# Projection stage cut on two engines, values 17 wide, and the first two attention units scored inside it

## The reference

```python
qkv = einsum('bysd,ed->byse', x, w_qkv) + b_qkv      # 8 batches, 512 tokens, 16 heads of 16
q, k, v = split(qkv.reshape(B, S, 16, 48).transpose(0, 2, 1, 3), 3, axis=-1)
attn = softmax(einsum('bhqd,bhkd->bhqk', q, k) / sqrt(16), axis=-1)
vals = einsum('bhqk,bhkd->bhqd', attn, v)
out  = vals.transpose(0, 2, 1, 3).reshape(B, S, 256) @ w_out.T + b_out
```

## Time and profile before

| what | value |
|---|---|
| runs | 1296.78 us median of 3 (1296.37 to 1297.04) |
| profiled execution | 1293.25 us, its span 1291.2 us |
| mean granted TensorE clock | 0.962 |
| projection: first matmul, last matmul on qk or values | 12.27 us, 98.5 us |
| attention: first score by query, first score by key | 109.60 us, 130.78 us |
| end of attention's last TensorE work | 520.9 us |
| the rest (recurrence, routing, experts) | to 1291.2 us |

### The profile page before, as it was taken

How to read it: one execution, slowest core, us unless ns; L and a number is a source line. 1 busy time by engine, 2 the same in 40 slices (tenths; PEclk the granted TensorE clock), 3 DMA queues, 4 the chain that set the end, 5 groups by cost and what they waited for, 6 DMA issues and landing times. The chain is left out here.

```text
span 1291.2 us, 21179 instructions
## 1 busy us (share of the span) xinstructions
PE 1179.1 (91%) x5606; PEld 704.0 (55%) x5607; DVE 832.4 (64%) x1458; ACT 496.1 (38%) x867; POOL 404.7 (31%) x520
## 2 busy tenths in 40 slices
PE   6996999999999999767999999982999999999996
PEld 3652233333333332454566665551888888888885
DVE  4998788888888883367777788856333433333332
ACT  2430777777777778211212121242122222222221
POOL 1021431101101110211444333446344554455443
PEclk9996999999999999878999999996999999999999
DMA  9885233333333321022334323311133333333332
GB/s 287 309 275 184 71 99 93 103 96 96 100 92 97 103 85 34 33 55 77 98 98 97 70 51 75 82 34 33 30 53 49 49 51 55 49 49 49 53 53 33
DMA packets 108674, 113.04 MB, mean 88 GB/s; under 512 B 26080, under 2 KB 97904, under 8 KB 107600
## 3 DMA queue, kind: packets, MB, share of 16 engines
q1 hardware_dynamic: 90528, 89.05, 24.0%
q0 software_dynamic: 18112, 23.57, 10.6%
HBM read 68.81 MB, written 43.62 MB: 87 GB/s over the span
## 5 line engine op out<-in xcount | busy, mean ns | idle before, releaser
L637 DVE TENSOR_REDUCE neg_max<-by_query 128x2 f32<-128x1024 f32 x256 | 301.3, 1219 | 62.5 <-PE by_query L538 61.7
L696 ACT ACTIVATE k_wu_e<-by_key 128x512 f32<-128x512 f32 x512 | 277.2, 600 | 83.5 <-PE by_key L546 80.0
L546 PE MATMUL by_key<-k_wg_e 99*128 99x512 bf16 x512 | 179.2, 384 | 3.8 <-ACT k_wu_e L696 2.1
L538 PE MATMUL by_query<-k_wg_e 96*128 96x512 bf16 x512 | 160.4, 396 | 11.3 <-PEq L106 7.5
L1407 POOL DMA_INDIRECT out_rows<-y,slot x72 | 113.2, 1572 | 182.9 <-DVE y L1544 179.9
L1500 ACT ACTIVATE gate<-ps_up 128x512 f32<-128x512 f32 x72 | 43.2, 600 | 304.4 <-PE ps_up L72 304.4
L1460 PE MATMUL ps_y<-k_wd_e,acts_T 128*128 x576 | 136.1, 379 | 0.8 <-ACT acts_T L1509 0.8
L557 PE MATMUL pv<-k_wu_e,k_wd_e 128*32 128x512 f32 x1024 | 136.2, 604 | 0.2 <-ACT k_wu_e L696 0.2
L546 PEld LDWEIGHTS by_key<-k_wg_e 99*128 99x128 bf16 x512 | 41.9, 97 | 145.3 <-ACT k_wu_e L696 84.6
L1460 PEld LDWEIGHTS ps_y<-k_wd_e,acts_T 128*128 128x128 f32 x576 | 109.1, 190 | 18.6 <-issue 1.0
L1528 DVE CAST x_T<-ps_x 128x256 fp32r<-128x256 f32 x72 | 30.6, 424 | 107.6 <-PE ps_x L1434 107.6
(11 more groups left out here) (211 smaller groups left out, 1906.8 us busy)
## 6 DMA issues: line engine op xcount, KB each, us to landing
k_wg_e<-kept_qk SPq DMA_DIRECT2D x384, 64.0 KB, 2.2
kept_qk<-qk_parts SPq DMA_DIRECT2D x32, 384.0 KB, 3.4
kept_v<-v_ones SPq DMA_DIRECT2D x8, 1024.0 KB, 5.8
k_wd_e<-kept_v SPq DMA_DIRECT2D x32, 256.0 KB, 3.0
k_wu_e<-in_xT POOLq DMA_DIRECT2D x8, 512.0 KB, 4.4
kept_heads<-k_wd_e SPq DMA_DIRECT2D x8, 512.0 KB, 3.0
k_heads_in<-kept_heads SPq DMA_DIRECT2D x8, 512.0 KB, 7.0
k_wg_e<-in_wg_e SPq DMA_DIRECT2D x8, 512.0 KB, 8.3
```

The costliest lines, as they stand in the source:

```text
L538: pe.matmul(by_query[:, pair_bank(b, g, k // 2) + k % 2, :], q_rows[0:KROWS, g, h, t * P:(t + 1) * P], k_rows[0:KROWS, g, h, :], start=Tru ...
L546: pe.matmul(by_key[:, key_bank(job), :], k_rows[0:SROWS, g, h, kt * P:(kt + 1) * P], q_rows[0:SROWS, g, h, :], start=True, stop=True).then ...
L637: dve.tensor_reduce(neg_max[:, g % 2, 2 * n:2 * n + 2], by_query[:, bank:bank + 2, :], AX.X, ALU.max, negate=True).then_inc(query_read, 1)
L696: act.activation(probs[:, key_tile(j) // 2 * G + j // 2 % G, j % 2, :], by_key[:, key_bank(job), :], ACT.Exp, scale=float(HD) ** -0.5).the ...
```

## The change

- **Cut on two engines.** ACT adds the bias and writes the bf16 high part straight from PSUM (`high_part`). DVE subtracts it in one instruction from the tile in PSUM plus bias (`rest`), ACT casts the middle part (`middle_part`), and DVE subtracts for the low part (`low_part`). Each engine works on tile j while it ends tile j - 1. Per tile ACT has two instructions and DVE two.
- **Values 17 wide.** A head has 16 values and one column of ones. In PSUM a head still has its 32 rows; DVE clears that bank once at the start of attention.
- **Units 0 and 1.** SP loads unit g (12 row loads spread behind the four q, k stores, the values last) in batch 2 + g. In batches 4 to 7 TensorE scores four pairs of units 0 and 1 per batch, between its own tiles, into the two banks `fold_ps`, one pair at a time: each pair but a unit's first waits until DVE has taken the maxima of the one before. The split, turn and placing of unit 0's maxima are in the projection stage as well, and the split of unit 1's.
- **Moved.** x is loaded before POOL's fills, and the rows of ones in k_rows are set at the start. The fold and the frequencies come between batches 3 and 4, and TensorE waits there until ACT has copied the fold. The wait for all stores is now the first act of SP in the attention stage. The powers on POOL go into attention's units 0 to 3, ahead of each unit's split.

The core of the diff:

```diff
-VW = 2 * HD
+VW = HD + 1
+PV_ROWS = 32
@@ stage_qkv, gpsimd
+            for par in range(2):
+                load_x(0, par)
             pool.memset(v_ones[:, :, :, :], 1.0).then_inc(ones_set, 1)
+            pool.memset(mem["max_parts"][:, :, :], 0.0).then_inc(ones_set, 1)
+            pool.wait_ge(ones_set, 2)
+            pool.memset(mem["k_rows"][KROWS:SROWS, :, :, :], 1.0).then_inc(ones_set, 1)
...
+            for g in range(2):
+                pool.wait_ge(pair_read, PAIRS * (g + 1))
+                if g == 1:
+                    pool.wait_ge(first_turned, 1)
+                split_max(pool, mem, neg_max[:, g, :], first_split, 4 * g, first_step)
+                if g == 0:
+                    pool.wait_ge(first_copied, 1)
+                    place_max(pool, mem, 0)
@@ stage_qkv, sync
+                    if unit is not None:
+                        for n in range(ROW_LOADS // 4 * j, ROW_LOADS // 4 * (j + 1)):
+                            load_rows(sp, mem, dram, 0, unit, n)
...
+            for g in range(NG):
+                store(2 + g, g)
             store(B - 2)
             store(B - 1)
-            for j in range(4):
-                sp.wait_ge(parts_stored[j], 16 * B)
-            sp.wait_ge(v_stored, 16 * B)
@@ stage_qkv, tensor
+        PAIR_BATCH = B - 4
+        BEHIND_QK, BEHIND_V = {B - 4: (1, 2), B - 3: (0, 2), B - 2: (2, 3), B - 1: (0, 2)}, (0, 2)
+            def score_pair(b, n):
+                g, n = divmod(TT * (b - PAIR_BATCH) + n, PAIRS)
+                if n == 0:
+                    pe.wait_ge(unit_in[g], 16 * LOADS)
+                if g == 1 and n == 0:
+                    pe.wait_ge(first_copied, 1)
+                elif n:
+                    pe.wait_ge(pair_read, PAIRS * g + n)
+                for k in (2 * n, 2 * n + 1):
+                    h, t = k // TT, k % TT
+                    mm = pe.matmul(fold_ps[:, k % 2, :], q_rows[0:KROWS, g, h, t * P:(t + 1) * P],
+                                   k_rows[0:KROWS, g, h, :], start=True, stop=True)
+                mm.then_inc(pair_scored, 1)
...
+                    if pairs and j in BEHIND_QK[b]:
+                        score_pair(b, BEHIND_QK[b].index(j))
...
+                    if pairs and t in BEHIND_V:
+                        score_pair(b, len(BEHIND_QK[b]) + BEHIND_V.index(t))
@@ stage_qkv, scalar
+            def high_part(b, j):
+                act.wait_ge(parts_stored[j], 16 * b)
+                act.wait_ge(qk_made, 4 * b + j + 1)
+                act.activation(qk_parts[:, j, 0, :], qk_ps[:, j, :], ACT.Identity,
+                               bias=bqk[:, j:j + 1]).then_inc(high_made, 1)
+            def middle_part(b, j):
+                act.wait_ge(qk_out[j], b + 1)
+                act.activation(qk_parts[:, j, 1, :], qk_rest[:, j, :], ACT.Copy).then_inc(middle_made, 1)
+                for j in range(1, 4):
+                    high_part(b, j)
+                    middle_part(b, j - 1)
@@ stage_qkv, vector
+            def rest(b, j):
+                dve.wait_ge(cut[j], b)
+                dve.wait_ge(high_made, 4 * b + j + 1)
+                dve.scalar_tensor_tensor(qk_rest[:, j, :], qk_ps[:, j, :], bqk[:, j:j + 1], qk_parts[:, j, 0, :],
+                                         ALU.add, ALU.subtract).then_inc(qk_out[j], 1)
+            def low_part(b, j):
+                dve.wait_ge(middle_made, 4 * b + j + 1)
+                dve.tensor_tensor(qk_parts[:, j, 2, :], qk_rest[:, j, :], qk_parts[:, j, 1, :],
+                                  ALU.subtract).then_inc(cut[j], 1)
+                rest(b, 0)
+                for j in range(1, 4):
+                    rest(b, j)
+                    low_part(b, j - 1)
+                    if pairs and j == BEHIND_QK[b][0] + 1:
+                        take_pair(b, 0)
+                low_part(b, 3)
+                if pairs:
+                    take_pair(b, 1)
+                dve.wait_ge(v_stored, 16 * b)
+                for t in range(TT):
...
+                    if pairs and t == 1:
+                        take_pair(b, 2)
+                if pairs:
+                    take_pair(b, 3)
@@ stage_attention
-            for g in range(2):
-                pe.wait_ge(unit_in[g], 16 * LOADS)
-                for k in range(G * TT):
-                    score_by_query(0, g, k)
-                    if g == 1 and k == 3:
-                        turn_max(0, 0)
+            pe.wait_ge(pv_zeroed, 1)
             for g in range(NG):
                 unit(0, g)
-                    mm = pe.matmul(pv[VW * h:VW * (h + 1), :], v_unit[:, g, kt, h, :],
+                    mm = pe.matmul(pv[PV_ROWS * h:PV_ROWS * h + VW, :], v_unit[:, g, kt, h, :],
-            for g in range(2):
-                for n in range(G * TT // 2):
-                    take_max(0, g, n)
+            dve.memset(pv[:, :], 0.0).then_inc(pv_zeroed, 1)
```

More of the change, by code:

```diff
@@ L170, in _, with store @@
             sp.dma_start(dram["out"][ROWS:ROWS + P, :], mem["zeros"][:, :]).then_inc(filled, 16)
-            def store(b):
+            def store(b, unit=None):
                 for j in range(4):
@@ L180, in store @@
                              v_ones[:, :, :, :].rearrange("p t h w -> p (t h w)")).then_inc(v_stored, 16)
-            with sp.Fori(0, B - 2) as b:
-                store(b)
+                if unit is not None:
+                    load_values(sp, mem, dram, 0, unit)
+            store(0)
+            store(1)
             for j in range(4):
@@ L228, in _ @@
             mm.then_inc(folded, 1)
-            pe.wait_ge(qk_out[0], B)
-            pe.matmul(qk_ps[:, 0, 0:1], sine[:, :], a_col[:, :], start=True, stop=True).then_inc(omega_made, 1)
+            pe.wait_ge(qk_out[3], PAIR_BATCH)
+            pe.matmul(qk_ps[:, 3, 0:1], sine[:, :], a_col[:, :], start=True, stop=True).then_inc(omega_made, 1)
+            pe.wait_ge(fold_copied, 2)
+            for i in range(PAIR_BATCH // 2, B // 2):
+                for par in range(2):
+                    project(i, par)
         @block.scalar
@@ L245, in _ @@
                 act.wait_ge(folded, n + 1)
-                act.activation(mem[name][:, :, :], fold_ps[:, n, :].rearrange("p (m n) -> p m n", m=2), ACT.Copy)
+                act.activation(mem[name][:, :, :], fold_ps[:, n, :].rearrange("p (m n) -> p m n", m=2),
+                               ACT.Copy).then_inc(fold_copied, 1)
+            for b in range(PAIR_BATCH, B):
+                high_and_middle(b)
         @block.vector
@@ L257, in _ @@
             dve.wait_ge(ones_set, 1)
-            with dve.Fori(0, B // 2) as i:
-                for par in range(2):
[L260 to L281, removed]
@@ L485, in _, with unit @@
-            for g in range(NG):
-                place_max((g + 1) // NG, (g + 1) % NG)
-                b2, g2 = (g + 2) // NG, (g + 2) % NG
-                split_max(b2, g2)
-                for k in ((4, 5), (6, 7), (8,), (9,))[g]:
-                    raise_powers(pool, link, mem, turned_by, k)
-            with pool.Fori(1, LAST) as b:
-                batch(b)
-            batch(LAST)
+                place_max(pool, mem, g)
+            def unit(b, g, powers):
+                b1, g1 = b + (g + 1) // NG, (g + 1) % NG
+                if not (isinstance(b1, int) and b1 > LAST):
+                    place(b1, g1)
+                for k in powers:
+                    raise_powers(pool, link, mem, turned_by, k)
+                b2, g2 = b + (g + 2) // NG, (g + 2) % NG
+                if not (isinstance(b2, int) and b2 > LAST):
+                    split(b2, g2)
@@ L495, in _ @@
+            link = chain(pool, power_step, 0)
+            for g in range(NG):
+                unit(0, g, ((0, 1, 2), (3, 4, 5), (6, 7), (8, 9))[g])
+            with pool.Fori(1, LAST) as b:
+                for g in range(NG):
+                    unit(b, g, ())
+            for g in range(NG):
+                unit(LAST, g, ())
         @block.sync
```

281 lines of the change are left out of this document (154 added, 127 removed).

## The result

| | before | after |
|---|---|---|
| median of 4 runs, us | 1296.57 (1295.59 to 1297.04) | 1308.82 (1307.17 to 1310.37) |
| ratio, 95% interval | 1 | 1.0095 (1.0078 to 1.0113) |
| profiled execution, its span, us | 1293.25, 1291.2 | 1310.37, 1308.0 |
| mean granted clock | 0.962 | 0.961 |
| first score by key, us | 130.78 | 149.39 |

The change costs 12.3 us, 0.95%. The forecast was 1308.6. The median agrees, the parts less well: in the profiled execution the first score by key is 18.6 us later, not 11.8.

The account below looks back on a forecast made before the run. It took TensorE and DVE as both full in the projection loop. +5.8 us at the first score by key, +1 DMA and +5 clock made +11.8 on 1293.25: 1305, or 1308.6 on the median's scale, range 1290 to 1327.

Parts of the forecast that it names:

- Values 17 wide: Value products in attention: narrower loads into the array taken at 0, down to -4 us over the 128 blocks.
- start: TensorE's wait for x and weights: first matmul at 7.8 us instead of 12.27, bounds 6.0 and 9.6.
- cold first matmuls: First 16 matmuls of the projection: slow as before, +1.55 us.
- fold, uncovered: Between batches 3 and 4: TensorE waits for the fold, which before ran beside DVE's tail, +4.25 us.
- batches 4 to 7: Projection with pairs between tiles: 41.3 us of tiles, 6.9 of pairs and 29.2 of waits.
- into attention: End of projection to first score by key: last take 2.1 us, split 1.3, change of stage 0.5, pv clearing 0.4.
- DMA: Batches 2 and 3: row loads between stores make a store late and hold ACT, +1 us, bounds 0 and 4.
- Waits: Batches 4 to 7: TensorE waits for DVE's takes and ACT's copy of the turned maxima, 29.2 us in all.
- Clock: Batches 4 to 7: more than half of five long idles cost a spell at 1.2 GHz, +5 us, bounds 0 and 15.
- The takes don't hold TensorE: Rival, batches 4 to 7: DVE takes each pair once scored, the 29.2 us of waits go, 1274 us; chance 0.13.
- A clock that stays low: Rival, batches 4 to 7: the clock stays low throughout, 1340 us; chance 0.08.
- Tiles not side by side: Rival, attention: a block of eight 17-column matmuls takes 3.4 us instead of 1.0, near 1600 us; chance 0.02.

Follow-up runs that it names:

- takes_early: The changed kernel with only DVE's takes of the pairs' maxima moved ahead in its list: 1274.59 us, ratio 0.9846.
- x_late: The changed kernel with x loaded behind POOL's fill of v_ones again, as before: 1313.06 us, ratio 1.0082.
- clock_held: The changed kernel with TensorE recomputing a value tile where it would wait for a take in batches 4 to 7: 1302.92 us, ratio 1.0061.
- values_32: The changed kernel with values 32 columns wide a head again: 1313.56 us, ratio 1.0091.
- all_four: The changed kernel with early takes, fold behind batch 7, later loads held, unit 1's split in attention, pv bank cleared beside first scores: 1281.43 us, ratio 0.9829.
- fill_first: The kernel before with the fill of k_rows moved to the start, behind the first two loads of x: 1298.02 us, ratio 0.9961.
- loads_held: The changed kernel with early takes, and SP's later loads held back until the first x has landed: 1283.92 us, ratio 0.9857.
- fold_last: The changed kernel with early takes, and the fold and frequencies computed behind batch 7 in qk_ps: 1279.58 us, ratio 0.9822.

## Why the prediction was right, and where its terms were off

The mechanism was right: it is the order of DVE's list, and takes_early shows it. The sizes were off, and in this execution mostly one way. The value 144.16 below is the start of the last value tile and its 0.86 us (143.30 + 0.86).

| step | forecast, us | after, us | what it adds |
|---|---|---|---|
| start | 7.8 | 10.08 | +2.3 |
| cold first matmuls | +1.55 | +2.5 (9.36 against 6.87) | +0.9 |
| batches 0 to 3 | 10.32 each | 10.32 each | 0 |
| fold, uncovered | 4.25 | 4.30 (58.15 - 53.85) | 0 |
| batches 4 to 7 | 77.4 + clock 5 | 86.0 (58.15 to 144.16) | +3.6 |
| into attention | 4.3 | 5.2 (144.16 to 149.39) | +0.9 |
| DMA | +1 | 0 | -1.0 |
| sum | 142.6 | 149.39 | +6.7 (6.8 by the event) |

- **Start.** The upper bound, 9.6, supposed that weights that had landed by 6.01 would not be late. They came at 9.62 (x_late shows the steps between); the bound left the second transfer out. In all five kernels with early takes TensorE starts between 9.55 and 10.30.
- **Cold first matmuls.** From the first matmul to the first value tile the twelve profiled executions take 8.41 us (before) to 9.94 (takes_early), and the same kernel 9.94 and 8.53. So the 0.9 lies within what two executions of one kernel differ by.
- **Waits.** Forecast 29.2 in 15 waits, measured 24.7 in 14 (23.1 + 1.6), about 27 with the modelled drain of 0.16 us that lies ahead of each. The single ones sit where they were foreseen: 3.43 for the second pair of batches 4 and 6, 1.71 for it in batches 5 and 7, 3.35 and 3.36 for the third pair, 1.60 for the turned maxima. The fourth pairs' came at 0.41 to 0.92 (forecast 1.3) because slow tiles covered part of them: they are 1.19 in clock_held. At a clock of 1.00 the waits of the four batches cost 30.2 us (78.7 in clock_held less 48.5 of own work in takes_early), against the forecast's 29.2.
- **Clock.** The mis-sized term of this execution: +5 forecast, +7.3 measured (86.0 less the 78.7 of clock_held). In x_late and values_32 it is +3.8 and +4.9, so 5 lies among what the executions show, and 7.3 is the most. In after, own work was 86.0 - 27 = 59 us, against 48.2 worked out and 51.1 - 2.3 - 0.3 = 48.5 in takes_early: some 10 us of slow tiles, of which about 3 lay in time that would else have been waited. Behind each of the five waits of 2.77 to 3.43 us the pair or the tiles next to it ran slow, about 2 us for each; behind the nine of 0.27 to 1.71 us the pair kept its 0.59 to 0.61 us. I had let only some of the five count, at 1.55 each. The rule that the prediction cited, the Trainium skill (TensorE: Matmul & The Clock Gate, section "HAM oscillation — how this bites in real kernels"), would have had all five pay, and +8. The trace of after agrees with it. Those of x_late and values_32 do not: there full speed follows two of the five (66.52 and 73.06 in x_late, 67.31 and 94.81 in values_32). What decides it stays open.
- **Into attention.** Last take and split as forecast (2.1, 1.34); the change of stage took 1.25 us (147.60 to 148.85), not 0.5, and the clearing 0.54, inside its bounds.
- **DMA.** Batches 0 to 3 kept 10.32. ACT waited for stores (4.8 us in all), with the slack for it.
- **DVE's new instruction** is 0.75 us (row L392), my upper bound.
- **Values 17 wide.** Eight take 1.05 us against 1.06. From the first score by key to the last copy out of pv, attention is 388.6 us against 388.8: nothing, as forecast.
- **Why the median came out all the same.** Of the 6.8 us too few at the event, 1.5 came back behind it: the profiled executions differ by 17.1 where the event differs by 18.6. The other 4.9 are where these two executions lie: before's 3.3 under its median, after's 1.55 above. x_late and values_32, with the same order of tiles and takes, have the event at 145.04 and 146.85, 2.4 and 4.3 above the forecast's 142.6. The part behind the event, the same work in all, takes between 1158.2 us (takes_early) and 1169.8 (all_four) in the profiled executions. So the landing on 1308.6 to 0.2 us is luck.
- **Rivals.** "The takes don't hold TensorE" was priced at 1274, and takes_early, where that is made true, ran in 1274.6; in the kernel as changed the waits were above its 22 us. A clock that stays low fell: 0.74 to 1.00 in the windows, not 0.50. Tiles not side by side fell (1.05 us). The DMA bound fell for this kernel, but stores are what DVE or ACT waited for next in fill_first, loads_held and all_four.

What stays open: when a wait costs the clock, what paces x and the weights at the start, how much fold_last is worth in the median, and by how much a kernel that spaces the row loads between the stores otherwise would gain. None was tried further.

## What to carry to other kernels

Where two in-order engines hand one buffer back and forth, put the consumer's instruction in its list at the point where its input is ready, not behind work that needs the producer's next output: one engine's order was worth 31 to 37 us here, more than the rest of the change. Price a wait on TensorE at more than its length, with what the tiles behind it may lose to the clock: nothing to about 2 us for a wait of 3.4 us here. When a transfer is moved ahead, ask which one it delays: here x landed 2.2 us earlier and the weights 3.6 us later. And look at two executions of one kernel before you explain a few us at an event.

## What the runs showed of the hardware that was not expected

- Keeping TensorE busy with results that nobody reads made four batches 3.8 to 7.3 us shorter, although it still waited 11.4 us for DVE.
- The same waits of 3.35 and 3.43 us were followed by half speed in one execution and by full speed in another (after, x_late).
- A store's issue behind 12 row loads is 7.1 us late (0.59 each), and that shows only once the compute engine ahead of it is faster (fill_first).
- Holding the later loads back for 10 us gave x nothing and cost a batch 1.4 us.
